# The round of ones gets a PE step of its own in an attention and gated-MLP layer, with a fourth buffer for pair sums

## The chip, the cores and the metric

One core of one Trainium2 chip runs the whole layer. The metric is device time in microseconds, the median of several executions. PE is TensorE (matmuls), PEld its weight loads, ACT ScalarE, DVE VectorE, POOL GpSimd, SP SyncE, which here only issues DMAs.

## The reference, cut to what matters

```
x  = hidden_states                      # (2, 1024, 1024) f32
xn = layernorm(x)
q, k, v = bitnet_linear(xn, ...)        # 32 query heads of 32, 8 key and value heads
scores = q @ k.T / sqrt(32)
attn   = softmax(scores, axis=-1)
out    = bitnet_linear(attn @ v, o_weight, o_scale)
ffn    = (silu(xn @ gate) * (xn @ up)) @ down     # weights dequantised, inner size 3584
return x + out + ffn
```

The change is in the part from `scores` to `attn @ v`. A softmax divides by the sum of the exponentials over the keys, and that sum is what this text calls the denominator.

## The kernel before, in words

**The whole.** Normalisation and the projections come first, then attention, the output projection and the gated MLP. Attention is cut into 32 units; a unit is one of 2 sequences, one of 8 key heads (with its 4 query heads) and one half (512) of the queries. `u` is a unit, and each unit has 16 steps, `k` = 0 to 15; `e = 16u + k` counts the 512 steps. In front of them stands a head start: maxima of rows are worked out 25 steps (`LEAD`) ahead of the exponentials that need them.

**One step on PE** (L1323 to L1342). Every step issues four f16 score matmuls of 512 columns: two of `row_scores` (L1238, as long as e + 25 < 512), whose maxima DVE takes from three banks of PSUM (L965), and two of `key_scores` (L1254), whose exponentials ACT takes from three other banks (L721) into `prob`, a ring of 8 slots of 128x1024 f32. A step with `e % 4 == 2` or `e % 4 == 0` then issues a round of `values` (L1265): four f32 matmuls, one for each 32-column strip of the array, which the profile shows as eight MATMULs. It multiplies two slots of `prob` by V and accumulates in bank 6.

**The denominators.** POOL adds two slots of `prob` into one of three buffers `duo` (`add_pair`, L520 to L525; L525 is the addition). Eight such sums are made in a unit, as four groups `j` of two. PE multiplies a group's two sums by a matrix of ones (`pair_sums`, L1268 to L1279, matmuls at L1277), again as four strips, which adds over the partitions into bank 7. This is the round of ones. It is issued in the steps with `e % 4 == 0`, `e >= 8`, right behind that step's round of values, and takes the group of (e - 8). `add_pair` number n waits until the round of ones has read sum n - 3 (semaphore `dn_pe`) and until ACT has made both slots.

**Steps around it.** At k = 7 PE transposes the next unit's maxima into bank 7 (`maxima_rows`, L1245), which waits for the last unit's denominators to be out of that bank, and DVE splits them (L974, L976). ACT copies the numerators out at its step 1 (`evacuate_values`, L728), which the first round of values of the unit (k = 2) waits for, and the denominators at its step 5 (`evacuate_sums`, L734). SP then gathers the denominators with four small DMAs (`compact_sums`, L330), queued ahead of the load of the maxima (L318). DVE inverts them at its step 10 (L980), SP stores them (L336) and spreads them (L341), POOL multiplies (L529) and later takes the low half (L534). POOL also issues a DMA that adds a block of MLP weights (L546) after every third pair sum; SP issues a preset for it every sixth step (L366).

**What sets the order.** All orders are written out by hand. Each engine works strictly through its own list and waits on semaphores; there is no planner.

The lines that say it best:

```
L1332  if e % 4 == 2:
           values(u, k // 2 - 1)
       elif e % 4 == 0 and e >= 4:
           t = e - 4
           values(t // 16, t % 16 // 2 + 1)
           if e >= 8:
               pair_sums((e - 8) // 16, (e - 8) % 16 // 4)
       elif k == 7 and u + 1 < UNITS:
           maxima_rows(u + 1)
```

Of the kernel before, what the change touches and what calls it, by code (L numbers as in the profile page):

```python
# [40 lines left out]
def duo_of(u, j, hp):  # L41
    return 8 * u + 2 * j + hp
# [67 lines left out]
def layer_kernel(nc, x, wq, sq, wk, sk, wv, sv, wo, so, gw, gz, gs, uw, uz, us, dw, dz, ds, out, zscr, wscr, yscr, kscr, vscr, rscr):  # L110
# [4 lines left out]
    add, sub, mult, amin, amax, iseq = ALU.add, ALU.subtract, ALU.mult, ALU.min, ALU.max, ALU.is_equal  # L115

    ctx = ExitStack()
    with ctx:
# [3 lines left out]
        def sem(name):  # L122
            return ctx.enter_context(nc.semaphore(name))
# [5 lines left out]
        zone_b = zone[:, 64 * 256:139 * 256]  # L129

        def view(zone, kb, words, dt=f32):
            v = zone[:, kb * 256:kb * 256 + words]
            return v if dt == f32 else v.bitcast(dt)
# [30 lines left out]
        prob = view(zone_b, 24, 8192).rearrange("p (n c) -> p n c", n=8)  # L164
        num = view(zone_b, 56, 1024).rearrange("p (n c) -> p n c", n=2)
        den = view(zone_b, 60, 1024).rearrange("p (n c) -> p n c", n=2)
        vst = view(zone_b, 68, 512).rearrange("p (n k d) -> p n k d", n=2, k=8)
        duo = [view(zone_b, kb, 1024) for kb in (12, 20, 64)]
        zone_d = zone_b[:, 74 * 256:75 * 256]
        mxs = zone_d[:, 0:64].rearrange("p (n h c) -> p n h c", n=2, h=2)  # L170
        mtop = zone_d[:, 64:80]
        ones = zone_d[:, 80:112]
# [55 lines left out]
        ps = ctx.enter_context(nc.psum_tensor("ps", [P, 8, 512], f32))  # L228

        def bank16(b):  # L230
            return ps[:, b, :].bitcast(f16)
# [17 lines left out]
        s = {n: sem(n) for n in names}  # L249
# [245 lines left out]
        def _(pool):  # L495
# [24 lines left out]
            def add_pair(u, j, hp):  # L520
                n, e = duo_of(u, j, hp), 16 * u + 4 * j + hp
                pool.wait_ge(s["exp_ok"], 2 * (e + 3))
                if n >= 3:
                    pool.wait_ge(s["dn_pe"], (n - 3) // 2 + 1)
                nc.gpsimd.tensor_tensor(duo[n % 3], prob[:, e % 8, :], prob[:, (e + 2) % 8, :], add).then_inc(s["sum_ok"], 1)  # L525

            def divide(u):
                pool.wait_ge(s[f"rb_in{u % 2}"], 64 * (u // 2 + 1))
# [19 lines left out]
            for u in range(UNITS):  # L548
                for j in range(4):
                    for hp in range(2):  # L550
                        add_pair(u, j, hp)
                        n = duo_of(u, j, hp)
                        if n % 3 == 2 and n // 3 < TILES:
                            add_weights(n // 3)
                    if u >= 2 and j == 0:
                        divide(u - 2)
                    if u >= 2 and j == 2:
                        tail_of(u - 2)
# [38 lines left out]
        def _(act):  # L597
# [116 lines left out]
            def exp_step(e):  # L714
                if e >= 8:
                    u, kt = (e - 8) // 16, (e - 8) % 16 // 2
                    act.wait_ge(s["pv_pe"], round_of(u, kt) + 1)
                    act.wait_ge(s["sum_ok"], duo_of(u, kt // 2, e % 2) + 1)
                for m in (2 * e, 2 * e + 1):
                    act.wait_ge(s["st_pe"], m + 1)  # L720
                    A(prob[:, e % 8, m % 2 * 512:(m % 2 + 1) * 512], ps[:, 3 + m % 3, :], ACT.Exp,  # L721
                      scale=gam[:, 0:1]).then_inc(s["exp_ok"], 1)

            def evacuate_values(u):
                act.wait_ge(s["pv_pe"], round_of(u, 7) + 1)
                if u >= 2:
                    act.wait_ge(s["ol_ok"], u - 1)
                A(num[:, u % 2, :], ps[:, 6, :], ACT.Copy).then_inc(s["ev_ok"], 1)  # L728

            def evacuate_sums(u):  # L730
                act.wait_ge(s["dn_pe"], 4 * u + 4)
                if u >= 2:
                    act.wait_ge(s["mu_ok"], u - 1)
                A(den[:, u % 2, :], ps[:, 7, :], ACT.Copy).then_inc(s["evd_ok"], 1)  # L734

            def head_of(u):
                act.wait_ge(s["mu_ok"], u + 1)
                c0 = 512 * (u % 2)
                A(qz[:, u // 2, 0, c0:c0 + 512], num[:, u % 2, :], ACT.Copy).then_inc(s["oh_ok"], 1)
# [3 lines left out]
            for e in range(STEPS):  # L743
                u, k = e // 16, e % 16
                if e + 1 < STEPS:
                    exp_step(e + 1)
                if k == 1 and u:
                    evacuate_values(u - 1)
                if k == 5 and u:
                    evacuate_sums(u - 1)  # L750
                if k == 10 and u >= 2:
                    head_of(u - 2)
# [424 lines left out]
        def _(pe):  # L1177
            MM = nc.tensor.matmul
# [50 lines left out]
            def row_scores(i, half):  # L1229
                u = i // 16  # L1230
                if i % 16 == 0 and half == 0:
                    pe.wait_ge(s[f"q_in{u % 3}"], 192 * (u // 3 + 1))
                    if u % 2 == 0:
                        pe.wait_ge(s[f"k_in{u // 2 % 2}"], 48 * (u // 4 + 1))
                c = 2 * i + half
                if c >= 3:
                    pe.wait_ge(s["max_ok"], c - 2)
                MM(ps[:, c % 3, :], qst[0:96, u % 3, i % 16 // 4, i % 4 * P:(i % 4 + 1) * P],  # L1238
                   kst[0:96, u // 2 % 2, half * 512:(half + 1) * 512], start=True, stop=True).then_inc(s["s_pe"], 1)

            def maxima_rows(u):
                pe.wait_ge(s["top_ok"], u + 1)
                if u >= 2:
                    pe.wait_ge(s["evd_ok"], u - 1)
                TR(ps[0:16, 7, 0:P], mtop, id32[:]).then_inc(s["m_pe"], 1)  # L1245

            def key_scores(m):
                e, a = m // 2, m % 2
                u, kt, hp = e // 16, e % 16 // 2, e % 2
                if m % 32 == 0:  # L1250
                    pe.wait_ge(s[f"m_in{u % 3}"], 32 * (u // 3 + 1))
                if m >= 3:
                    pe.wait_ge(s["exp_ok"], m - 2)
                MM(ps[:, 3 + m % 3, :], kst[0:98, u // 2 % 2, kt * P:(kt + 1) * P],  # L1254
                   qst[0:98, u % 3, 2 * hp + a, :], start=True, stop=True).then_inc(s["st_pe"], 1)

            def values(u, kt):
                pe.wait_ge(s["exp_ok"], 2 * (16 * u + 2 * kt + 2))
                if kt == 0:
                    if u % 2 == 0:  # L1260
                        pe.wait_ge(s[f"v_in{u // 2 % 2}"], 16 * (u // 4 + 1))
                    if u:
                        pe.wait_ge(s["ev_ok"], u)
                for h in range(4):
                    last = MM(ps[32 * h:32 * h + 32, 6, :], vst[:, u // 2 % 2, kt, :],  # L1265
                              prob[:, (2 * kt + h // 2) % 8, h % 2 * 512:(h % 2 + 1) * 512], start=(kt == 0), stop=(kt == 7))
                last.then_inc(s["pv_pe"], 1)

            def pair_sums(u, j):
                n = duo_of(u, j, 0)  # L1270
                pe.wait_ge(s["sum_ok"], n + 2)
                if j == 0:
                    pe.wait_ge(s["mrow_ok"], min(u + 2, UNITS))
                    if u:
                        pe.wait_ge(s["evd_ok"], u)
                for h in range(4):
                    last = MM(ps[32 * h:32 * h + 32, 7, :], ones, duo[(n + h // 2) % 3][:, h % 2 * 512:(h % 2 + 1) * 512],  # L1277
                              start=(j == 0), stop=(j == 3))
                last.then_inc(s["dn_pe"], 1)  # L1279

# [43 lines left out]
            for e in range(STEPS):  # L1324
                u, k = e // 16, e % 16
                if e + LEAD < STEPS:
                    row_scores(e + LEAD, 0)
                if 2 * e + 3 < 2 * STEPS:
                    key_scores(2 * e + 3)
                if e + LEAD < STEPS:  # L1330
                    row_scores(e + LEAD, 1)
                if 2 * e + 4 < 2 * STEPS:  # L1332
                    key_scores(2 * e + 4)
                if e % 4 == 2:
                    values(u, k // 2 - 1)
                elif e % 4 == 0 and e >= 4:
                    t = e - 4
                    values(t // 16, t % 16 // 2 + 1)
                    if e >= 8:
                        pair_sums((e - 8) // 16, (e - 8) % 16 // 4)  # L1340
                elif k == 7 and u + 1 < UNITS:
                    maxima_rows(u + 1)  # L1342
            values(UNITS - 1, 7)
# [11 lines left out]
            for o in range(FQ):  # L1355
                last = TR(ps[:, 7, o * IT:(o + 1) * IT], snat_d[:, o * P:(o + 1) * P], id32[0:IT, 0:IT])
            last.then_inc(s["snat_pe"], 1)

            for i in range(FQ):
# [3 lines left out]
                for t in range(KT):  # L1363
                    last = TR(bank16(2 + i % 2)[:, t * P:(t + 1) * P], wosg[:, i % 2, t * P:(t + 1) * P], id16[:])
# [65 lines left out]
            for hf in range(HALVES):  # L1430
                for j in range(PAIRS):
                    if hf == 1 and j in TURNS:
                        n = 2 * TURNS.index(j)
# [43 lines left out]
```

## Time and profile before

| what | value |
|---|---|
| median of 3 runs | 2496.96 us (2495.53 to 2497.45) |
| the profiled execution | 2498.24 us, of which the span is 2496.4 us |
| granted TensorE clock, mean over the span | 0.977 |
| PE busy | 2371.1 us, 95% of the span |
| DVE, ACT, POOL busy | 1810.4, 1566.0, 996.7 us |
| attention (first to last round of values) | 308.7 to about 1146 us |

The profile is of one execution. Busy time says when an engine had an instruction in flight, not that it worked at its peak: PE's matmuls overlap, so PE's time is better read from the distance between the starts of two rounds. In the timeline a row merges like instructions that follow each other, and a bracket gives the idle time before it and what ended that idle time.

### The profile page before, as it was taken

How to read it: one execution, taken by the hardware profiler on the slowest of the kernel's cores; microseconds unless marked ns; L12 is line 12 of the kernel's file. 1: busy time of each engine (PE TensorE's matmuls, PEld its weight loads, DVE VectorE, ACT ScalarE, POOL GpSimd, SP SyncE). 2: the span in 40 equal slices, each digit the busy share in tenths (PEclk: the TensorE clock that was granted, in tenths of full speed). 3: DMA queues.
4: the chain of work that ended last, by engine and by line, in shares of the span. 5: the costliest groups of instructions: out<-in, count | busy, mean ns of one | idle time of the engine just before them, and what ended most of it. 6: DMA issues, size and time to landing. Idle time of an engine off the chain costs nothing.

```text
span 2496.4 us, 33125 instructions
## 1 busy us (share of the span) xinstructions
PE 2371.1 (95%) x12408; PEld 962.0 (39%) x12408; DVE 1810.4 (73%) x2326; ACT 1566.0 (63%) x2008; POOL 996.7 (40%) x553
## 2 busy tenths in 40 slices
PE   5698999999999999995999999999999999999998
PEld 3244333333333333322344444444444444444444
DVE  5577877777777777762547777777777777777777
ACT  5444377777777777784126666666665566666664
POOL 1111089999999999995002222221001222222000
PEclk9799899999999999997999999999999999999999
DMA  5201155555556555544121111113103111114111
GB/s 174 70 9 45 53 73 81 89 82 87 90 81 90 84 86 88 86 76 95 75 93 35 34 34 51 34 34 110 43 34 135 68 34 47 38 34 168 51 34 68
DMA packets 179851, 174.65 MB, mean 70 GB/s; under 512 B 87586, under 2 KB 127394, under 8 KB 179702
## 3 DMA queue, kind: packets, MB, share of 16 engines
q1 hardware_dynamic: 117430, 150.62, 19.1%
q0 software_dynamic: 62272, 22.03, 11.4%
q8 instruction: 95, 1.56, 0.3%
q14 instruction: 54, 0.44, 0.1%
HBM read 160.08 MB, written 65.45 MB: 90 GB/s over the span
## 4 chain that ended last, share of the span: by engine, by line
PE 90%; DVE 4%; issue 2%; ACT 1%; DMA 1%; POOL 1%; SPq 0%; DVEq 0%; ACTq 0%; POOLq 0%
PE ps L1394 31%; PE ps L1410 15%; PE ps L1238 10%; PE ps L1265 10%; PE ps L1254 9%; PE ps L1216 5%; PE ps L1277 4%; PE ps L1374 4%; POOL zone L525 1%; DVE zone L941 0%; PE ps L1426 0%; DMA zone<-in_L_attn_o_weight_dram 0%; PE ps L1202 0%; DVE zone L873 0%; PE ps L1194 0%
## 5 line engine op out<-in xcount | busy, mean ns | idle before, releaser
L1394 PE MATMUL ps<-xT,zone 128*128 128x512 f16 x3584 | 774.6, 379 | 3.6 <-DVE zone L1157 2.7
L965 DVE TENSOR_REDUCE zone<-ps 128x1 f32<-128x512 f32 x1024 | 638.7, 683 | 173.2 <-PE ps L1238 173.2
L721 ACT ACTIVATE zone<-ps,sm 128x512 f32<-128x512 f32 x1024 | 626.6, 691 | 182.0 <-PE ps L1254 180.1
L525 POOL TENSOR_TENSOR zone<-zone 128x1024 f32<-128x1024 f32 x256 | 633.4, 2584 | 176.7 <-ACT zone L721 103.6
L1134 DVE TENSOR_SCALAR ps<-ps,zone_c 128x1024 f32<-128x1024 f32 x392 | 506.8, 1293 | 161.4 <-PE ps L1394 159.3
L789 ACT ACTIVATE ps<-ps,zone_c 128x1024 f32<-128x1024 f32 x392 | 426.5, 1088 | 261.0 <-PE ps L1394 259.2
L1394 PEld LDWEIGHTS ps<-xT,zone 128*128 128x128 f16 x3584 | 350.2, 98 | 427.3 <-DVE zone L1157 4.2
L1238 PE MATMUL ps<-zone 96*128 96x512 f16 x1024 | 394.6, 388 | 5.1 <-DVE zone L965 4.6
L1254 PE MATMUL ps<-zone 98*128 98x512 f16 x1024 | 388.1, 382 | 4.1 <-ACT zone L721 4.0
L1410 PE MATMUL ps<-zone 128*128 128x512 f16 x1792 | 387.1, 379 | 0.0
L576 POOL CAST zone<-zone 128x1024 f16<-128x1024 f32 x56 | 58.0, 1037 | 724.5 <-DVE zone L1138 724.5
L1145 DVE TENSOR_SCALAR ps<-ps,zone_c 128x1024 f32<-128x1024 f32 x216 | 279.2, 1293 | 93.0 <-PE ps L1410 92.9
L803 ACT ACTIVATE ps<-ps,zone_c 128x1024 f32<-128x1024 f32 x216 | 235.0, 1088 | 137.8 <-PE ps L1410 137.8
L1265 PE MATMUL ps<-zone 128*32 128x512 f32 x2048 | 273.1, 605 | 2.1 <-ACT zone L721 0.5
L1410 PEld LDWEIGHTS ps<-zone 128*128 128x128 f16 x1792 | 175.4, 98 | 211.4
L1238 PEld LDWEIGHTS ps<-zone 96*128 96x128 f16 x1024 | 99.9, 98 | 326.9 <-DVE zone L965 233.6
L1216 PE MATMUL ps<-xT,zone 128*128 128x512 f16 x768 | 183.0, 397 | 1.2 <-ACT xT L606 1.2
L584 POOL TENSOR_TENSOR xT<-xT,zone 128x1024 f32<-128x1024 f32 x8 | 18.7, 2357 | 361.8 <-ACT zone L808 361.8
L1254 PEld LDWEIGHTS ps<-zone 98*128 98x128 f16 x1024 | 99.5, 98 | 108.1 <-ACT zone L721 20.0
L1277 PE MATMUL ps<-zone 128*32 128x512 f32 x1024 | 134.2, 596 | 4.3 <-POOL zone L525 4.3
L937 DVE TENSOR_SCALAR zone<-zone 128x512 f32<-128x512 f32 x80 | 37.8, 473 | 126.4 <-ACT zone L774 57.6
L578 POOL TENSOR_TENSOR zone<-zone 128x1024 f16<-128x1024 f32 x56 | 119.1, 2127 | 11.8 <-issue 7.4
(127 smaller groups left out, 1358.3 us busy)
## 6 DMA issues: line engine op xcount, KB each, us to landing
zone<-dequantised SPq DMA_DIRECT2D x84, 512.0 KB, 3.6
dequantised<-zero_points SPq DMA_DIRECT2D x84, 256.0 KB, 4.1
zone<-zone SPq DMA_DIRECT2D x384, 32.0 KB, 2.3
zone<-_attn_hidden_states_dram SPq DMA_DIRECT2D x16, 512.0 KB, 8.2
zone<-inverse_sums SPq DMA_DIRECT2D x128, 64.0 KB, 2.2
attention<-zone SPq DMA_DIRECT2D x32, 256.0 KB, 2.0
xT<-attention SPq DMA_DIRECT2D x4, 2048.0 KB, 12.0
dequantised<-in_L_ffn_gate_w_dram POOLq DMA_DIRECT2D x28, 256.0 KB, 6.2
```

The lines of the kernel that those rows point to most:

```text
L525: nc.gpsimd.tensor_tensor(duo[n % 3], prob[:, e % 8, :], prob[:, (e + 2) % 8, :], add).then_inc(s["sum_ok"], 1)
L721: A(prob[:, e % 8, m % 2 * 512:(m % 2 + 1) * 512], ps[:, 3 + m % 3, :], ACT.Exp, scale=gam[:, 0:1]).then_inc(s["exp_ok"], 1)
L789: A(pair, pair, ACT.Copy, scale=tab[:, t, 0, g:g + 1]).then_inc(s["act_ok"], 1)
L965: V.tensor_reduce(mxs[:, u % 2, half, i % 16:i % 16 + 1], ps[:, (2 * i + half) % 3, :], AX, amax).then_inc(s["max_ok"], 1)
L1134: V.tensor_scalar(pair, pair, tab[:, t, 1, g:g + 1], None, mult).then_inc(s["dve_ok"], 1)
L1145: V.tensor_scalar(pair, pair, dtab[:, it, o:o + 1], None, mult).then_inc(s["dve_ok"], 1)
L1216: last = MM(ps[:, output_bank(n), :], wT[:, kt, f * P:(f + 1) * P], xT[:, b2, part, kt, s2 * 512:(s2 + 1) * 512], start=(kt == 0 and part ...
L1238: MM(ps[:, c % 3, :], qst[0:96, u % 3, i % 16 // 4, i % 4 * P:(i % 4 + 1) * P], kst[0:96, u // 2 % 2, half * 512:(half + 1) * 512], start= ...
L1254: MM(ps[:, 3 + m % 3, :], kst[0:98, u // 2 % 2, kt * P:(kt + 1) * P], qst[0:98, u % 3, 2 * hp + a, :], start=True, stop=True).then_inc(s[" ...
L1265: last = MM(ps[32 * h:32 * h + 32, 6, :], vst[:, u // 2 % 2, kt, :], prob[:, (2 * kt + h // 2) % 8, h % 2 * 512:(h % 2 + 1) * 512], start= ...
L1394: last = MM(ps[:, 4 * s2 + 2 * m + c, :], ring[:, buf, m * H + g * P:m * H + (g + 1) * P], xT[:, hf, part, g, c * 512:(c + 1) * 512], star ...
L1410: last = MM(ps[:, 4 * s2 + 2 * m + c, :], ring[:, k % RING, (it % 4) * 512 + o * P:(it % 4) * 512 + (o + 1) * P], hT[:, it, part, c * 512: ...
```

## The change: what it does

`pair_sums` leaves the step of a round of values (`e % 4 == 0`) and is issued one step further on (`e % 4 == 1`, e >= 9), behind that step's four score matmuls. A fourth buffer joins `duo`, in space that attention did not use, so that `add_pair` number n waits for the reading of sum n - 4 and not n - 3. `evacuate_sums` moves from ACT's step 5 to its step 6. No instruction is added or taken away: rounds, additions and DMAs stay as many, and SP's and POOL's lists keep their order.

```
-        duo = [view(zone_b, kb, 1024) for kb in (12, 20, 64)]
+        duo = [view(zone_b, kb, 1024) for kb in (12, 20, 64, 70)]
...
-                if n >= 3:
-                    pool.wait_ge(s["dn_pe"], (n - 3) // 2 + 1)
-                nc.gpsimd.tensor_tensor(duo[n % 3], prob[:, e % 8, :], prob[:, (e + 2) % 8, :], add).then_inc(s["sum_ok"], 1)
+                if n >= 4:
+                    pool.wait_ge(s["dn_pe"], (n - 4) // 2 + 1)
+                nc.gpsimd.tensor_tensor(duo[n % 4], prob[:, e % 8, :], prob[:, (e + 2) % 8, :], add).then_inc(s["sum_ok"], 1)
...
-                if k == 5 and u:
+                if k == 6 and u:
                     evacuate_sums(u - 1)
...
-                    last = MM(ps[32 * h:32 * h + 32, 7, :], ones, duo[(n + h // 2) % 3][:, h % 2 * 512:(h % 2 + 1) * 512],
+                    last = MM(ps[32 * h:32 * h + 32, 7, :], ones, duo[(n + h // 2) % 4][:, h % 2 * 512:(h % 2 + 1) * 512],
...
                     values(t // 16, t % 16 // 2 + 1)
-                    if e >= 8:
-                        pair_sums((e - 8) // 16, (e - 8) % 16 // 4)
+                elif e % 4 == 1 and e >= 9:
+                    pair_sums((e - 9) // 16, (e - 9) % 16 // 4)
```

## Rows read from the trace of the kernel before

**Rows 1.** Busy time by stretch: two steady stretches of attention, then its end

```profile
core 0: us, PE busy (x) PEld busy (x) DVE busy (x) ACT busy (x) POOL busy (x), PEclk, DMA share, GB/s
360.00:460.00 100.00, 99.81 (x609) 30.26 (x607) 78.61 (x139) 78.97 (x134) 90.63 (x48) 1.00 0.58 86
...
960.00:1060.00 100.00, 99.81 (x614) 30.25 (x607) 77.63 (x136) 77.61 (x131) 91.11 (x49) 1.00 0.56 88
...
1106.50:1155.00 48.50, 37.61 (x230) 8.43 (x228) 3.42 (x9) 34.64 (x59) 45.29 (x25) 0.94 0.35 46
```

**Rows 2.** Timeline of PE, steps 1 to 10 of one unit, the rounds and their neighbours

```profile
700.79 1.06 PE L1265 MATMUL ps<-zone 128*32 128x512 f32 x8
...
702.64 0.39 PE L1238 MATMUL ps<-zone 96*128 96x512 f16 x1
...
704.18 0.38 PE L1254 MATMUL ps<-zone 98*128 98x512 f16 x1
...
704.61 1.06 PE L1265 MATMUL ps<-zone 128*32 128x512 f32 x8
...
707.45 1.07 PE L1265 MATMUL ps<-zone 128*32 128x512 f32 x8
707.91 0.13 PEld L1277 LDWEIGHTS ps<-zone 128*32 128x32 f32 x4 [0.30 <-issue]
...
710.85 0.38 PE L1254 MATMUL ps<-zone 98*128 98x512 f16 x1
...
711.16 0.16 PEld L1265 LDWEIGHTS ps<-zone 128*32 128x32 f32 x8 [0.37 <-issue]
711.16 1.06 PE L1265 MATMUL ps<-zone 128*32 128x512 f32 x8
...
712.15 0.10 PEld L1238 LDWEIGHTS ps<-zone 96*128 96x128 f16 x1 [0.84 <-issue]
...
714.11 1.07 PE L1265 MATMUL ps<-zone 128*32 128x512 f32 x8
...
717.82 1.06 PE L1265 MATMUL ps<-zone 128*32 128x512 f32 x8
```

**Rows 3.** Timeline, same stretch: ACT, DVE, POOL and SP beside it

```profile
702.89 2.36 POOL L525 TENSOR_TENSOR zone<-zone 128x1024 f32<-128x1024 f32 x1 [0.76 <-PE ps L1277]
703.07 2.48 DVE L965 TENSOR_REDUCE zone<-ps 128x1 f32<-128x512 f32 x4 [1.22 <-PE ps L1238]
...
703.87 0.59 ACT L728 ACTIVATE zone<-ps 128x512 f32<-128x512 f32 x1
...
710.54 0.59 ACT L734 ACTIVATE zone<-ps 128x512 f32<-128x512 f32 x1
...
711.02 4.21 ACT L721 ACTIVATE zone<-ps,sm 128x512 f32<-128x512 f32 x7
711.15 2.44 SPq L330 DMA_DIRECT2D zone<-zone  x4
...
718.80 0.24 DVE L980 RECIPROCAL zone<-zone 128x16 f32<-128x16 f32 x1
```

**Rows 4.** The rounds of ones by stretch, steady part and end (PE busy, eight MATMULs each)

```profile
310.00:1106.50 796.50, 124.95 (x960) 31.21 (x960) 1.00 0.55 84
1106.50:1155.00 48.50, 9.22 (x64) 2.02 (x64) 0.94 0.35 46
```

**Rows 5.** Who waited for whom between 360 and 1060 us: total, times, longest

```profile
POOL zone L525 <- PE ps L1277: 60.4, 66, 2.0
...
PEld ps L1277 <- POOL zone L525: 3.9, 13, 0.3
```

**Rows 6.** The gathering DMAs of the denominators, L330: issue to landing

```profile
DMA to landing us min/median/max: 1.7/2.2/5.1
```

**Rows 7.** Timeline of POOL at the end of attention

```profile
1112.42 4.94 POOL L525 TENSOR_TENSOR zone<-zone 128x1024 f32<-128x1024 f32 x2
1118.55 2.36 POOL L525 TENSOR_TENSOR zone<-zone 128x1024 f32<-128x1024 f32 x1 [1.19 <-PE ps L1277]
...
1146.36 4.80 POOL L525 TENSOR_TENSOR zone<-zone 128x1024 f32<-128x1024 f32 x2
```

## The prediction, made before the changed kernel had run

> **What bounds the kernel now.** I read the busy time by stretch first. Over attention's steady part PE is busy 99.81 of every 100 us at the full granted clock (1.00, the 2.4 GHz level), POOL about 91, ACT and DVE under 80 [rows 1]. Only at the end, from about 1106 us, where the row scores have run out, does PE fall to 37.61 of 48.50 us while POOL has 45.29 [rows 1]. So the steady part is PE's and the end is POOL's. A busy PE need not be an efficient one, so I then read the timeline for the distance between starts. Two steps have eight score matmuls and one round of values. Without ones that takes 707.45 - 704.61 = 2.84 us; with a round of ones behind the values it takes 711.16 - 707.45 = 3.71 us [rows 2]. The pattern repeats with these distances through all steady units, with two exceptions a unit: 704.61 - 700.79 = 3.82 us where the numerators are copied out, and 714.11 - 711.16 = 2.95 us where the maxima are transposed [rows 2]. Last I read the waits, to see what the present order costs: POOL waits much for the round of ones (60.4 us in 700), PE hardly for POOL (3.9 us, never over 0.3) [rows 5].
>
> **The round on its own, the main term.** No matmul is added, but it now stands between four scores and four scores. Seven score distances take 704.18 - 702.64 = 1.54 us, 0.22 each, so eight take 1.76 [rows 2]. The rest of the 2.84 is what a lone round of values costs: 1.08 us. A round of ones behind values costs 3.71 - 2.84 = 0.87. Both rounds are eight f32 MATMULs of 128x512 on 32-column strips, so a lone round of ones should cost what a lone round of values does: 0.21 more by this pair of rows; with the other plain pair (717.82 - 714.11 = 3.71, half of rounding each way) 0.21 to 0.25. The seam is visible. The last score starts at 710.85 and the round at 711.16, 0.31 later where two scores are 0.22 apart, and its weight loads start with it, not under the score; behind the round PEld sits for 0.84 us until the next score's weights load at 712.15, though nothing that the profile shows holds it ("issue"). Between values and ones no such seam shows: the ones' weights load at 707.91, in the middle of the values [rows 2]. I take 0.23 us a round. The lower bound of this price is 0, if a seam beside four scores can hide; the upper one 0.36, the excess of the dearest distance of the timeline (3.82 against 2.84, less 0.87, is 0.11 for a wait, added to 0.25). I take 0.23 since the lone round of values is the same shape in the same surroundings. There are 960 / 8 = 120 rounds in the steady stretch [rows 4]: 120 x 0.23 = **+27.6 us**. The 8 rounds of the end [rows 4] lie where PE has room (37.61 of 48.50) and cost nothing there; if the cover were gone, 1.8 us.
>
> The seam's nature is not in the rows. TensorEngine Tiling in the Trainium skill, Key Properties, says that a change of tiling mode drains the TensorE; by that rule every lone round pays twice, going in and coming out, which speaks against this change as the rows do. A rule for it is on the page TensorE: Matmul & The Clock Gate of the Trainium skill (Architectural detail: the array is 16x 32x32): the queue can pull weight loads ahead of matmuls in flight. If that held across the seam the main term would be 0; the rows show it holding between scores and from values to ones, but not from scores to a round.
>
> **The wait for the numerators goes.** ACT copies them out at 703.87 to 704.46 and the round of values at 704.61 stands behind it, which makes that distance 3.82 instead of 3.71: 0.11 us [rows 2, 3]. In the new order a lone round of ones (about 1.1 us) stands between the scores of step 1 and those of step 2, so the copy is done in time. 30 units have it in the steady stretch: 30 x 0.11 = **-3.3 us**.
>
> **The scores' engines.** DVE takes 0.62 us for a maximum (2.48 / 4), ACT 0.60 for an exponential (4.21 / 7) [rows 3]: two of either fit in 1.24 us, and a step with a round has 0.88 + 1.1 = 1.98 us, so both idle a little in each step instead of 1.22 us in one go (DVE's wait at 703.07). That idle time costs nothing, since neither bounds. The tight spot is the run of eight scores (steps 3 and 4, 7 and 8, ...), where the fourth row score needs the first one's maximum. It is entered with all three banks free, before and after; nothing changes.
>
> **ACT's copy of the denominators, one step later.** It would have waited at step 5 for a round of ones now issued in that step; at 6 it doesn't. Queued behind it are the exponentials of the run of eight scores. The copy takes 0.59 us [rows 3] in a step of 1.98 us with 1.20 us of exponentials, so it ends before the second score of the run is there: 0. If the cover were gone: 0.59 a unit, 18 us in all, an upper bound. PE's transpose at step 7 waits for this copy too; I put it about 1 us behind the copy: 0.
>
> **The chain from the denominators to the inverse.** In time from the step-4 round of values, the copy ended at 711.13 - 707.45 = 3.7 us and will end near 4.8 (one lone round more, 1.1). SP issues its four DMAs at once (2.44 us) and they land in 2.2 us at the median, 5.1 at most [rows 3, 6]. So they are in at 9.5. DVE's reciprocal stands at 718.80 - 707.45 = 11.35 [rows 3] and moves to about 11.6: 2 us of slack, where there were near 3. SP's load of the maxima queues behind the four DMAs and slips by about 1 us; it is first used six steps (about 9 us) later. Cost 0.
>
> **POOL and the fourth buffer.** The second addition of a group waited for the previous round of ones ([0.76 <-PE ps L1277] at 702.89 [rows 3]). With four buffers it waits for a round two groups back, which is long past, so it runs as soon as ACT is ready. In the steady part this frees up to 60 us of POOL's waiting, worth nothing since PE does not wait for POOL (3.9 us in 700 [rows 5]; I count none of it back). At the end it is worth something: POOL adds without a break from 1118.55 to 1151.16, with one wait of 1.19 us just before [rows 7], and all of the later work follows it. POOL enters this end two to three us ahead, since its addition no longer stands behind the round, and loses the 1.19: **-3.5 us**, between 0 (no lead carried over) and -6 (its wait and the whole lead of a few steps).
>
> **Sum.** +27.6 - 3.3 - 3.5 = +20.8 us. Against the profiled execution (2498.24: 2496.4 of span and 1.8 around it) that gives 2519.0. That execution stands 1.3 us above the median of the runs, so I predict **2518 us**. What follows attention only shifts with it.
>
> **Rivals.**
> *The seam hides (faster).* If weights for a lone round load under the scores, or the drain costs nothing between fours, the place is each seam at `e % 4 == 1` and the price 0: -3.3 - 3.5 = -6.8, so 2490 us. It decides below 0.06 us a round, where 120 rounds no longer outweigh 6.8 us. For it speaks only that no row shows a seam with four scores on either side; against it, that each lone round of values in the trace pays, with nothing to wait for. Chance 0.06.
> *The seam is partly hidden:* half of 0.23 gives +13.8 - 6.8 = +7.0, 2504 us. Chance 0.07, of which a third lands within 5 us of before.
> *A new wait on top of it.* The denominators' copy delays exponentials in the run of eight scores, or a late landing (5.1 us at most [rows 6] against 2 + 2.2) holds DVE at its reciprocal and PE at its row scores. At half of 0.59 a unit, 30 units: +9, 2527 us; at the whole, 2536 us. Against it is the room computed above. Chance 0.09.
> *The change does nothing:* PE works in program order and the line is moved, so this has no way to happen beyond the partly hidden case.
>
> **How the numbers follow.** The forecast has 0.78. Its own range is 2512 to 2525, from a seam of 0.20 to 0.26 and the end's 0 to -6. The range that should hold 8 in 10 reaches into half of the neighbours: **2508 to 2528**. Two runs of this kernel can be told apart at about 0.2%, 5 us. Faster has the first rival: 0.06. Within 0.2%: 0.03. Slower: the forecast, most of the partly hidden case and the new wait, 0.91.
>
> **What would show it.** In the changed trace, distances between rounds of values: 2.84 us for a pair of steps without ones as before, 1.76 + 2 x 1.08, near 3.93 us, for a pair with, and no 3.82 next to 3.71 any more. A round of ones should start 0.31 us behind the last score, its weight loads with it. POOL's waits for L1277 should fall to nearly nothing in the steady part, ACT's and DVE's idle time should split into shorter pieces, PE stay at 99.8% busy. The last pair sum should come after the steady part's end sooner by some 3 us. The prediction is wrong if the pair with ones stays at 3.71, or if L980 or L721 appear as what PE waits for.

## The result and the profile after

The changed kernel takes **2518.64 us** (median of 4 runs, 2518.07 to 2519.18), the kernel before beside it 2496.67 (4 runs, 2495.53 to 2497.45). The ratio is 1.0089, with a 95% interval of 1.0073 to 1.0105: slower by 22.0 us, where 2518 was predicted.

Busy time by stretch of the changed kernel, two steady stretches and the end of attention (columns as in [rows 1]):

```profile
360.00:460.00 100.00, 100.00 (x592) 26.76 (x592) 77.17 (x135) 78.34 (x130) 88.93 (x48) 1.00 0.53 81
960.00:1060.00 100.00, 100.00 (x596) 26.76 (x592) 77.26 (x135) 78.23 (x129) 89.04 (x48) 1.00 0.55 86
1130.00:1180.00 50.00, 36.31 (x225) 6.85 (x225) 2.19 (x8) 33.81 (x57) 42.11 (x23) 0.90 0.41 61
```

PE is busy all the time, a little more than before, and does less: 592 MATMULs in 100 us against 609 [rows 1], at the same granted clock. The share of busy time would call this an improvement. The time is lost inside "busy"; the lower count of MATMULs hints at it, and the distances between starts show where it goes.

Timeline of the changed kernel, PE and its neighbours, from a run of scores over a round of ones to the round of values behind it:

```profile
737.29 1.06 PE L1265 MATMUL ps<-zone 128*32 128x512 f32 x8
...
738.95 0.38 PE L1254 MATMUL ps<-zone 98*128 98x512 f16 x1
739.26 0.16 PEld L1277 LDWEIGHTS ps<-zone 128*32 128x32 f32 x8 [0.43 <-issue]
739.26 1.06 PE L1277 MATMUL ps<-zone 128*32 128x512 f32 x8
739.52 0.59 ACT L728 ACTIVATE zone<-ps 128x512 f32<-128x512 f32 x1
...
740.25 0.10 PEld L1238 LDWEIGHTS ps<-zone 96*128 96x128 f16 x1 [0.84 <-DVE zone L965]
740.26 0.39 PE L1238 MATMUL ps<-zone 96*128 96x512 f16 x1
...
740.50 2.36 POOL L525 TENSOR_TENSOR zone<-zone 128x1024 f32<-128x1024 f32 x1 [2.10 <-PE ps L1277]
...
741.23 0.16 PEld L1265 LDWEIGHTS ps<-zone 128*32 128x32 f32 x8 [0.43 <-issue]
741.23 1.07 PE L1265 MATMUL ps<-zone 128*32 128x512 f32 x8
```

The round of ones starts 0.31 us behind the last score, where two scores are 0.22 apart, and the next score follows 1.00 us behind the round's start. Its weights load with it, not ahead. The distance of the two rounds of values is 741.23 - 737.29 = 3.94 us where it was 3.71 [rows 2], and this pair of steps also holds the copy of the numerators (L728, done at 740.11), for which PE waited before (3.82 us). Now it is done 1.1 us early.

How long attention's parts last is read from the first start of the values (L1265), the last start of the row scores (L1238) and the last start of the ones (L1277). The changed kernel, then the kernel before (duration in ns min/median/max, first and last start in us):

```profile
L1238 PE MATMUL ps<-zone x1024: 377/380/634, 229.5 to 1129.4; 96*128 96x512 f16 x171
L1265 PE MATMUL ps<-zone x2048: 592/593/796, 305.7 to 1164.8; 128*32 128x512 f32 x187
L1277 PE MATMUL ps<-zone x1024: 592/605/1060, 316.5 to 1171.1; 128*32 128x512 f32 x171
```

```profile
L1238 PE MATMUL ps<-zone x1024: 377/379/634, 232.5 to 1107.1; 96*128 96x512 f16 x171
L1265 PE MATMUL ps<-zone x2048: 589/593/949, 308.7 to 1145.5; 128*32 128x512 f32 x187
L1277 PE MATMUL ps<-zone x1024: 592/592/1062, 318.6 to 1152.1; 128*32 128x512 f32 x171
```

The steady part (first round of values to last row score) grew from 1107.1 - 308.7 = 798.4 to 1129.4 - 305.7 = 823.7 us, by **25.3**. The end (last row score to last MATMUL of ones) shrank from 45.0 to 41.7, by **3.3**. Together +22.0, as much as the difference of the medians. The two profiled executions are only 19.8 us apart (2518.07 and 2498.24): attention begins 3.0 us sooner in the changed one, before anything that the change touches, and the other 0.8 us lie behind attention. Over all the profiled executions of this study attention begins between 304.8 and 308.7 us, and what follows it varies by 2 to 3 us more. That the medians agree with the parts to 0.1 us is therefore in part luck.

### The profile page after: what moved, and what is told of

The parts are those of the page before. It is cut to its first block, busy times and chain, and to the rows that moved or that the text cites. A ratio compares the mean times of both kernels' runs of the same rounds, so it can differ in the third digit from the quotient of the medians.

```text
span 2515.8 us, 33124 instructions
## 1 busy us (share of the span) xinstructions
PE 2396.6 (95%) x12408; PEld 938.0 (37%) x12408; DVE 1818.8 (72%) x2326; ACT 1584.3 (63%) x2008; POOL 998.1 (40%) x553
## 4 chain that ended last, share of the span: by engine, by line
PE 90%; DVE 4%; issue 2%; POOL 1%; ACT 1%; DMA 1%; SPq 0%; DVEq 0%; ACTq 0%; POOLq 0%
PE ps L1394 31%; PE ps L1410 15%; PE ps L1238 10%; PE ps L1265 10%; PE ps L1254 9%; PE ps L1277 5%; PE ps L1216 5%; PE ps L1374 4%; POOL zone L525 1%; DVE zone L941 0%; PE ps L1426 0%; DMA zone<-in_L_attn_o_weight_dram 0%; PE ps L1202 0%; DVE zone L873 0%; PE ps L1194 0%
## 5 line engine op out<-in xcount | busy, mean ns | idle before, releaser
L965 DVE TENSOR_REDUCE zone<-ps 128x1 f32<-128x512 f32 x1024 | 647.0, 683 | 189.3 <-PE ps L1238 189.2
L721 ACT ACTIVATE zone<-ps,sm 128x512 f32<-128x512 f32 x1024 | 644.7, 688 | 185.9 <-PE ps L1254 185.3
L1238 PE MATMUL ps<-zone 96*128 96x512 f16 x1024 | 395.8, 389 | 5.1 <-DVE zone L965 4.6
L1265 PE MATMUL ps<-zone 128*32 128x512 f32 x2048 | 272.7, 605 | 0.0
L1238 PEld LDWEIGHTS ps<-zone 96*128 96x128 f16 x1024 | 99.9, 98 | 404.5 <-DVE zone L965 311.4
L1277 PE MATMUL ps<-zone 128*32 128x512 f32 x1024 | 137.2, 608 | 4.0 <-POOL zone L525 4.0
L578 POOL TENSOR_TENSOR zone<-zone 128x1024 f16<-128x1024 f32 x56 | 119.1, 2127 | 11.6 <-issue 7.2
```

Source lines behind the costliest of these rows:

```text
L965: V.tensor_reduce(mxs[:, u % 2, half, i % 16:i % 16 + 1], ps[:, (2 * i + half) % 3, :], AX, amax).then_inc(s["max_ok"], 1)
```

## The experiments

Two theories at first. *The seam*: each stretch of strip matmuls between full-width ones costs PE 0.24 us beyond its passes, whatever stands in it, and the change makes 120 stretches more. *The rhythm*: the lateness of the round, the moved copy or the new order of supply to ACT and DVE costs, and the seam is a symptom. "Steady" and "end" below are as above, from each run's own profile. The expectations count the end to the end of the last round (46.1 us before, 42.8 in the changed kernel), the table to the start of its last MATMUL (45.0 and 41.7).

| kernel | median us | ratio to before (95%) | steady | end |
|---|---|---|---|---|
| before | 2496.3 to 2496.7 | | 798.4 | 45.0 |
| the change | 2518.64 | 1.0089 (1.0073 to 1.0105) | 823.7 | 41.7 |
| e1_own_step_three | 2522.79 | 1.0105 (1.0089 to 1.0120) | 824.0 | 45.3 |
| e2_fourth_only | 2493.59 | 0.9987 (0.9978 to 0.9996) | 798.5 | 42.0 |
| e3_every_second | 2507.17 | 1.0047 (1.0034 to 1.0061) | 813.1 | 41.7 |
| e4_full_width | 2491.42 | 0.9983 (0.9974 to 0.9992) | 794.9 | 41.6 |
| e5_joined_again | 2490.29 | 0.9976 (0.9966 to 0.9987) | 794.3 | 43.1 |
| e6_numerators_early | 2492.54 | 0.9985 (0.9976 to 0.9994) | 794.7 | 45.1 |
| e7_joined_dve_end | 2485.41 | 0.9959 (0.9945 to 0.9973) | 794.4 | 40.2 |

**The two parts of the change, one at a time.** The first keeps the own step and the moved copy and takes the fourth buffer out (diff against the changed kernel); the second adds only the buffer to the kernel before.

```
-        duo = [view(zone_b, kb, 1024) for kb in (12, 20, 64, 70)]
+        duo = [view(zone_b, kb, 1024) for kb in (12, 20, 64)]
...
-                if n >= 4:
-                    pool.wait_ge(s["dn_pe"], (n - 4) // 2 + 1)
+                if n >= 3:
+                    pool.wait_ge(s["dn_pe"], (n - 3) // 2 + 1)
...
```

> The changed kernel without the fourth buffer: the round of ones in its own step, three buffers. If the seam is the whole cost, a pair of steps with ones takes 3.95 us as in the changed kernel, 120 x 0.24 - 30 x 0.11 = +25.5 us in the steady part. POOL's second addition then waits for the previous group's round, one step later than before the change, so its work begins the end of attention late: the end keeps its 46.1 us or gets up to 3 us longer. Total before + 25 to + 29, about 2523 us. Rival (the step only works with four buffers): PE waits for POOL's sums in the steady part, the pair is longer than 3.95 us and the time is over 2530.

> The kernel before with the fourth buffer alone. Seam theory: PE's distances stay 2.84, 3.71, 3.82 and 2.95 us; POOL starts its additions earlier, which is worth something only in the end (46.1 us before, 42.8 in the changed kernel): -1 to -4 us in all, about 2494. Rival (the fourth buffer costs, through the place of its memory or more POOL traffic beside DVE and ACT): the steady distances grow and the time is above 2500.

The parts add up. The own step alone makes the steady part 25.6 us longer and leaves the end as it was (45.3), 2522.79 us. The buffer alone leaves the steady part (798.5) and takes 3.0 us off the end, 2493.59 us; its interval of the ratio lies just below 1, and the place of the saving in the profile is what makes it credible. So the change is a loss of 25.6 and a gain of about 3 in one.

A little of the 3.0 is not POOL's. PE's last round of ones, in the kernel before and then with the buffer alone:

```profile
1151.22 1.94 PE L1277 MATMUL ps<-zone 128*32 128x512 f32 x8 [4.29 <-POOL zone L525]
```

```profile
1144.86 1.07 PE L1277 MATMUL ps<-zone 128*32 128x512 f32 x8 [1.69 <-POOL zone L525]
```

PE had idled 4.29 us in one case and 1.69 in the other, and the round took 1.94 us (the granted clock was 0.75 between 1145 and 1153 us) against 1.07. Read to the start of the round, the end is 1151.22 - 1107.1 = 44.12 before and 1144.86 - 1103.3 = 41.56 with the buffer alone, 2.6 us less. In the changed kernel the last round takes 1.93 us as before, so its 3.3 is not touched by this.

**A dose.** Every second round goes back behind the values of the step before:

```
                     values(t // 16, t % 16 // 2 + 1)
+                    if e >= 8 and e % 8 == 0:
+                        pair_sums((e - 8) // 16, (e - 8) % 16 // 4)
-                elif e % 4 == 1 and e >= 9:
+                elif e % 8 == 5 and e >= 9:
                     pair_sums((e - 9) // 16, (e - 9) % 16 // 4)
```

> The changed kernel with every second round of ones (groups 0 and 2 of a unit) back behind the values of the step before, the others in a step of their own. Half the lone rounds: if each lone round costs 0.24 us by itself, 60 x 0.24 = 14.4 less than the changed kernel. The round that stood between steps 1 and 2 of a unit is a lone one still (group 2 of the unit before is joined at its step 0, group 3 is alone at its step 5): so step 1 has none, and the wait for the numerators comes back, +3.3. Total 2518.6 - 14.4 + 3.3 = 2507.5 us. Rival (the cost is one of rhythm, an uneven supply of scores, not one per lone round): not half way; near 2497 or near 2519.

2507.17 us, and a steady part of 813.1: 14.7 us over before where 60 x 0.24 = 14.4 makes the forecast. The timeline of its rounds shows both kinds side by side:

```profile
705.97 1.07 PE L1265 MATMUL ps<-zone 128*32 128x512 f32 x8
706.85 1.04 PE L1277 MATMUL ps<-zone 128*32 128x512 f32 x8
709.79 1.06 PE L1265 MATMUL ps<-zone 128*32 128x512 f32 x8
712.63 1.06 PE L1265 MATMUL ps<-zone 128*32 128x512 f32 x8
714.61 1.07 PE L1277 MATMUL ps<-zone 128*32 128x512 f32 x8
716.58 1.06 PE L1265 MATMUL ps<-zone 128*32 128x512 f32 x8
```

The joined round starts 0.88 us behind the values and makes 709.79 - 705.97 = 3.82 us with the wait for the numerators, which is back; the lone one makes 716.58 - 712.63 = 3.95.

**Late, but joined.** Four buffers and the copy at step 6 as in the change; the round two steps beyond its old place, in front of the values there:

```
                 if e % 4 == 2:
+                    if e >= 10:
+                        pair_sums((e - 10) // 16, (e - 10) % 16 // 4)
                     values(u, k // 2 - 1)
...
-                elif e % 4 == 1 and e >= 9:
-                    pair_sums((e - 9) // 16, (e - 9) % 16 // 4)
```

> Four buffers and the copy of the denominators at ACT's step 6 as in the changed kernel, but the round of ones goes two steps beyond its old place, into the steps with e % 4 == 2, right in front of their round of values: late as in the changed kernel, yet with no strip round of its own. Seam theory: pairs of steps take 2.85 and 3.71 us again, the 3.82 goes (the ones run in front of the values that wait for the numerators, -3.3), the end is 0 to 3.5 shorter: 2490 to 2494 us. Rival (lateness or the moved copy costs, not the seam): stays at or above 2510.

2490.29 us. The rhythm theory falls here: this round is later than in the changed kernel, the copy sits where it sat, and the cost is gone. The steady part is 4.1 us under before. The numerators are 3.3 of it. The rest is a matter of counting: the last of the 120 rounds (0.87 us) now stands behind the last row score and falls to the end, which is 43.1 and not 42.

```profile
702.17 1.07 PE L1277 MATMUL ps<-zone 128*32 128x512 f32 x8
703.05 1.04 PE L1265 MATMUL ps<-zone 128*32 128x512 f32 x8
705.88 1.07 PE L1265 MATMUL ps<-zone 128*32 128x512 f32 x8
708.72 1.06 PE L1277 MATMUL ps<-zone 128*32 128x512 f32 x8
709.61 1.04 PE L1265 MATMUL ps<-zone 128*32 128x512 f32 x8
```

From one round of ones to the next 708.72 - 702.17 = 6.55 us, as 2.84 + 3.71 before; the changed kernel takes 2.85 + 3.94 = 6.79.

**What the seam is.** The round stays alone in its step, but the strips are replaced by one matmul with `ones_w`, a 128x128 matrix of ones:

```
-                for h in range(4):
-                    last = MM(ps[32 * h:32 * h + 32, 7, :], ones, duo[(n + h // 2) % 4][:, h % 2 * 512:(h % 2 + 1) * 512],
-                              start=(j == 0), stop=(j == 3))
+                last = MM(ps[:, 7, :], ones_w, duo[n % 4][:, 0:512], start=(j == 0), stop=(j == 3))
```

> The changed kernel with the four strip matmuls of a round of ones replaced by one f32 matmul over the whole width of the array (128x128 ones by 128x512), at the same place. It leaves out the denominators of three of the four heads and gives all of them that of the first. Two passes of 0.43 us each, if a full-width f32 matmul streams as the strips do, are the 0.86 us of a joined round. Theory A (the seam is paid for going from full-width matmuls to strips and back): no seam here, the ones' weights load under the last score, the round costs 0.86, a pair of steps with it 3.71 us, the time is 2518.6 - 120 x 0.24, near 2490. Theory B (the seam is paid at any change between f16 and f32 or at any round that waits on a semaphore): it stays, 3.95 us and 2518.

2491.42 us. PE in its timeline (L1240, L1256 are the scores, L1278 the one matmul of ones, L1267 the values):

```profile
705.82 0.38 PE L1256 MATMUL ps<-zone 98*128 98x512 f16 x1
706.04 1.02 PE L1278 MATMUL ps<-zone,zone_c 128*128 128x512 f32 x2
706.90 0.38 PE L1240 MATMUL ps<-zone 96*128 96x512 f16 x1
...
707.56 0.38 PE L1256 MATMUL ps<-zone 98*128 98x512 f16 x1
707.87 1.07 PE L1267 MATMUL ps<-zone 128*32 128x512 f32 x8
708.87 0.39 PE L1240 MATMUL ps<-zone 96*128 96x512 f16 x1
```

Same place, same f32, same wait on a semaphore, same two passes of 0.43 us. Going in takes 0.22 us, the distance of two scores, and coming out 0.86, the passes alone. The strips of L1267 a microsecond later take 0.31 and 1.00. So the seam is 0.09 on the way in and 0.14 on the way out, and belongs to the change between full width and strips. The steady part is 28.8 us under the changed kernel's, 120 x 0.24. TensorEngine Tiling in the Trainium skill (Key Properties) says that a change of tiling mode drains the TensorE; the run agrees in that each change costs time, 0.23 to 0.24 us here for both ways together. That it is a drain, no row shows by itself.

This run changes one thing more: the round has two MATMULs where the strips have eight, each with a weight load of its own. The number is not what costs, since the rounds of ones in the joined run have all eight and the next round starts 0.88 to 0.89 us behind them (703.05 - 702.17, 709.61 - 708.72).

The waits offer a second rival. Between 360 and 1060 us they put more of the weight loader's idle time on DVE; the kernel before, the changed kernel, full width:

```profile
PEld ps L1238 <- DVE zone L965: 190.0, 370, 0.8
```

```profile
PEld ps L1238 <- DVE zone L965: 251.0, 359, 0.8
```

```profile
PEld ps L1240 <- DVE zone L967: 196.8, 372, 0.8
```

The 61 us more go with the loader's 0.84 us behind a lone round, as at 740.25 above. The view puts that idle time down to DVE, but DVE's maxima had ended 0.25 us earlier (738.71 + 1.29 = 740.00). With the full-width round DVE's list and the order of the work are the same, all but 7 of the 61 us are gone, and so is the cost. DVE was not what PE waited for.

**The numerators by themselves.** The kernel before with `if k == 0 and u:` in front of `evacuate_values(u - 1)` in place of `k == 1`:

> The kernel before with one line moved: ACT copies the numerators out at its step 0, not 1, in the time in which it idles for scores behind the joined rounds. If the 3.82 us distance is only PE waiting for that copy, it becomes 3.71 in each of 30 units: -3.3 us, 2493. Rival (the copy now delays the exponentials behind it and PE waits for them): other distances grow, and the time is 2496 or more.

2492.54 us, steady 3.7 us shorter and the end the same. In its timeline the pair of steps with the copy in it takes 727.33 - 723.63 = 3.70 us. The wait of 0.11 us a unit was real and is removed by either means.

**What sets the end.** The joined kernel with one addition of each of the last seven groups on DVE, under a semaphore of its own:

```
+            def add_late(g):
+                n, e = 2 * g + 1, 4 * g + 1
+                dve.wait_ge(s["exp_ok"], 2 * (e + 3))
+                dve.wait_ge(s["dn_pe"], (n - 4) // 2 + 1)
+                V.tensor_tensor(duo[n % 4], prob[:, e % 8, :], prob[:, (e + 2) % 8, :], add).then_inc(s["evb_ok"], 1)
...
+                if e % 4 == 0 and e // 4 - 1 >= G0:
+                    add_late(e // 4 - 1)
...
```

`G0` is 121; POOL leaves these seven additions out, and the waits of PE and ACT are fitted to the new semaphore.

> The joined kernel (four buffers, ones in front of the values of e % 4 == 2) with the second addition of the last seven groups done by DVE, which has nothing left to do there. If POOL's additions set the end of attention, 7 x 2.9 = 20 us of them leave POOL, the bound goes to ACT (25 steps of 1.3 us, 33 us, and some 4 us behind them) and the end shrinks from 44 to about 37: 2490.3 - 7 = 2483 us. Rival (ACT or PE sets the end, or POOL and DVE slow each other): the end stays within 2 us of 44, 2488 to 2492.

2485.41 us, the fastest kernel of the study and 11 us under the kernel before. But the end shrank only from 43.1 to 40.2. In the way the expectation counts, to the end of the last round, that is from 44.0 to 40.8: neither the 37 expected nor the 42 to 46 of the rival. The medians are 4.9 us apart, the end's 2.9 is all of it that the profiles place. POOL had been the bound: now it waits for rounds of ones (L1307) seven times between 1100 and 1142 us, with three of these waits below. The chain that ended last between 1100 and 1145 us now runs through PE and ACT by turns (L1280 are the key scores, L738 the exponentials), and the key scores' weight loads wait for exponentials 26 times, 16.2 us in all. That this loop is what bounds now is read from the chain and not tried by a run. The additions on DVE (L1037) and POOL (L532):

```profile
1107.05 3.22 DVE L1037 TENSOR_TENSOR zone<-zone 128x1024 f32<-128x1024 f32 x1
...
1112.70 1.23 DVE L1037 TENSOR_TENSOR zone<-zone 128x1024 f32<-128x1024 f32 x1 [2.43 <-PE ps L1307]
...
1135.64 3.15 DVE L1037 TENSOR_TENSOR zone<-zone 128x1024 f32<-128x1024 f32 x1 [4.22 <-ACT zone L738]
```

```profile
1106.83 2.36 POOL L532 TENSOR_TENSOR zone<-zone 128x1024 f32<-128x1024 f32 x1 [2.71 <-PE ps L1307]
...
1112.74 3.40 POOL L532 TENSOR_TENSOR zone<-zone 128x1024 f32<-128x1024 f32 x1 [1.03 <-PE ps L1307]
...
1135.33 2.37 POOL L532 TENSOR_TENSOR zone<-zone 128x1024 f32<-128x1024 f32 x1 [0.57 <-PE ps L1307]
```

## Why the prediction was right, and where it was not

**The main term** (+27.6 predicted for 120 lone rounds) held: 0.24 us a round against 0.23, 28.8 us in all, by the distances, by the dose and by the full-width run. The reading from the lone round of values was a fair one since a round of ones is the same to PE.

**The numerators** (-3.3) held; the pair of steps is 3.94 with the copy in it as without, and e6 has the term alone at 3.7 less in the steady part.

**The end** (-3.5) measured -3.3, and e1 against the change shows that it is the fourth buffer's (45.3 against 41.7). POOL around the last row score, in the kernel before (last row score at 1107.1; the rows behind are in [rows 7]) and in the changed kernel (1129.4):

```profile
1106.00 2.36 POOL L525 TENSOR_TENSOR zone<-zone 128x1024 f32<-128x1024 f32 x1 [0.57 <-PE ps L1277]
1108.32 1.26 POOL L529 TENSOR_TENSOR zone<-zone 128x512 f32<-128x512 f32 x1
1109.54 2.37 POOL L525 TENSOR_TENSOR zone<-zone 128x1024 f32<-128x1024 f32 x1
```

```profile
1129.22 2.37 POOL L525 TENSOR_TENSOR zone<-zone 128x1024 f32<-128x1024 f32 x1 [0.87 <-PE ps L1277]
...
1132.10 2.65 POOL L525 TENSOR_TENSOR zone<-zone 128x1024 f32<-128x1024 f32 x1
1135.21 4.69 POOL L525 TENSOR_TENSOR zone<-zone 128x1024 f32<-128x1024 f32 x2 [0.46 <-ACT zone L721]
```

Its last wait before the unbroken run is 0.46 us, for ACT, where it was 1.19 for a round [rows 7]: 0.7 us less. The rest is the lead. Behind the last row score POOL starts 14 additions before and 13 in the changed kernel; the addition (2.4 us) and one multiplication (L529, 1.2 us) are already done, and against that the addition in flight ends 0.9 us later behind the score (2.2 against 1.3). That makes 2.7 us, the "two to three us ahead" of the prediction, and 3.4 in all by this estimate. So the term was right in its two parts, with the wait smaller than the 1.19 that it was put at. With three buffers in e1 it is 14 additions again.

**One step failed:** that with four buffers the addition "waits for a round two groups back, which is long past, so it runs as soon as ACT is ready", and with it the sign that POOL's waits for L1277 would fall to nearly nothing. Waits between 360 and 1060 us, the changed kernel:

```profile
POOL zone L525 <- PE ps L1277: 77.6, 74, 2.2
...
PEld ps L1277 <- POOL zone L525: 6.8, 16, 0.4
```

and the kernel before with the buffer alone:

```profile
POOL zone L525 <- ACT zone L721: 58.2, 64, 2.0
```

They rose from 60.4 [rows 5]. The round two groups back stood at step 4r of the group r's own steps, but the change moves it to 4r + 1, and there it ends behind the exponentials that the first addition needs; the addition starts when the round is over (740.50 behind L1277 at 739.26, in the timeline above). I counted the move for PE, ACT, SP and DVE and forgot it for POOL. With the round in its old place the wait is for ACT, as I had said, and L1277 is not among POOL's waits of that stretch at all. The wrong step cost nothing: PE's weight loads waited for POOL 6.8 us in 700, never over 0.4, and the pairs of steps with ones kept at 3.94 to 3.95 us. The gain at the end came all the same, since behind the last row score POOL is the slower one and the round two groups back is past.

**The covers** all held. In the changed kernel's timeline the copy of the denominators starts at 721.00, beside PE's round of values at 720.75, and the reciprocal follows:

```profile
721.00 0.59 ACT L734 ACTIVATE zone<-ps 128x512 f32<-128x512 f32 x1
...
721.62 2.43 SPq L330 DMA_DIRECT2D zone<-zone  x4
...
728.31 0.24 DVE L980 RECIPROCAL zone<-zone 128x16 f32<-128x16 f32 x1
```

From the round of values of step 4 (716.80) the copy ends 4.8 us later and the reciprocal stands at 11.5, as computed (4.8 and 11.6). In 700 us DVE waited for a landing once, for 0.3 us. The idle times split as forecast: DVE's 213 waits of up to 1.2 us for the row scores became 281 of up to 0.7, ACT's 132 of up to 1.4 for the key scores 308 of up to 0.7. And the round of values waits for exponentials (L721) no more than before: 11.1 us in 700 against 11.5.

## What to carry to other kernels

Count the stretches, not only the matmuls: where PE bounds, every group of strip matmuls between full-width ones cost 0.24 us more than its passes here (128x32 f32 strips between f16 scores, granted clock 1.00; other shapes were not run), so groups that can stand together should. Judge a reordering by the distance between two starts of the same instruction, since the busy share rose here while the kernel became slower. And when a buffer is added and its reader moved in the same edit, work out the new wait against the reader's new place.

## What the runs showed that I had not expected

A full-width f32 matmul of 128x512 shows as two MATMULs and takes 0.86 us from start to start, 0.43 each, and four strips of 32 columns together take nearly the same, 0.88 to 0.89 us where another strip round follows. Beside that only the way in and out is paid.

In the run with DVE's additions, those of 128x1024 f32 on DVE and POOL do not run side by side. DVE's takes 1.23 us if it begins first, and POOL's begun 0.04 us behind it then takes 3.40 instead of 2.36; begun 0.22 us behind POOL's, DVE's takes 3.22. Each time the later one is longer by about what the earlier one still had to do (1.04 us longer for 1.19 left, 1.99 for 2.14). It is likely one reason why handing seven additions to DVE gave 3 us and not 7: the last one (3.15 us at 1135.64, begun 0.31 behind POOL's) stands in the chain that ended last, ahead of the last round of ones, and is 1.9 us longer than 1.23. How the two engines exclude each other, the runs don't tell.
